# One core, AdaLN + FFN with low-rank experts: the sync engine's loop interleaves row stores with token loads

## What is computed

```python
base   = einsum('btd,od->bto', x, W)                       # conditional layer
logits = einsum('btd,ed->bte', x, Wr) + bias_of_language   # 8 experts, top 2, softmax -> gates
y      = base + 2.0 * einsum('bter,bte,eor->bto', einsum('btd,erd->bter', x, A), gates, B)
z      = einsum('bsi,oi->bso', y, Wf) + b                  # FFN layer
g2     = softmax(einsum('bsi,ei->bse', y, Wrf))            # 4 experts, dense mixture
out    = x + z + einsum('bse,bseo->bso', 2.0 * g2, lora(y))
```

## Time and profile before

| what | value |
|---|---|
| median of 3 runs | 323.39 us (323.33 to 323.43) |
| the profiled execution's own time | 323.47 us |
| its span, first to last instruction | 322.2 us |
| TensorE matmul busy | 318.4 us (99%) |
| VectorE busy | 262.6 us (82%) |
| ScalarE busy | 128.3 us (40%) |
| granted TensorE clock | full in all 40 slices of the span |
| data moved | 27.59 MB, mean 86 GB/s |

### The profile page before, as it was taken

The page is one execution under the profiler, slowest core; times in us unless marked ns, Lnnn a source line. Parts: engine busy times, 40 slices in busy tenths (PEclk is TensorE's granted clock), DMA queues, the critical chain, the costliest instruction groups (busy, mean ns, idle before and its releaser), DMA issues.

```text
span 322.2 us, 5996 instructions
## 1 busy us (share of the span) xinstructions
PE 318.4 (99%) x2246; PEld 312.1 (97%) x2246; DVE 262.6 (82%) x609; ACT 128.3 (40%) x258; POOL 11.3 (3%) x13
## 2 busy tenths in 40 slices
PE   8999999999999999999999999999999999999996
PEld 5999999999999899899999999999999999999996
DVE  4999999798799778988968968878895887888543
ACT  4872846495147236325412503421250350333111
POOL 1001003700000000000000000000000000000000
PEclk9999999999999999999999999999999999999999
DMA  7999000000000312700330150061024006002003
GB/s 273 414 404 287 4 2 0 2 0 2 0 2 0 132 24 46 259 3 0 108 155 1 62 199 0 0 195 65 0 73 187 0 18 241 1 0 110 24 0 130
DMA packets 10705, 27.59 MB, mean 86 GB/s; under 512 B 3167, under 2 KB 4703, under 8 KB 10689
## 3 DMA queue, kind: packets, MB, share of 16 engines
q1 hardware_dynamic: 10256, 26.83, 23.5%
q10 hardware_dynamic: 432, 0.53, 0.5%
HBM read 18.97 MB, written 8.39 MB: 85 GB/s over the span
## 4 chain that ended last, share of the span: by engine, by line
PE 97%; DMA 1%; DVE 0%; ACT 0%; SPq 0%; issue 0%
PE sums L1310 97%; DMA in<-part 1%; PE sums L1559 0%; DVE rows L1069 0%; DVE a_low L800 0%; ACT a_high L549 0%; SPq L444 0%
## 5 line engine op out<-in xcount | busy, mean ns | idle before, releaser
L1310 PE MATMUL sums<-b_high,a_high 128*128 128x256 f32 (+1 forms) x224 | 45.7, 288 | 0.4 <-DVE a_low L800 0.4
L1310 PE MATMUL sums<-b_low,a_high 128*128 128x256 f32 (+1 forms) x224 | 45.3, 285 | 0.0
L1310 PE MATMUL sums<-b_high,a_low 128*128 128x256 f32 (+1 forms) x224 | 45.2, 285 | 0.0
L1310 PEld LDWEIGHTS sums<-b_high,a_high 128*128 128x128 f32 x224 | 34.9, 190 | 1.1 <-DVE a_low L800 0.6
L1310 PEld LDWEIGHTS sums<-b_high,a_low 128*128 128x128 f32 x224 | 34.8, 189 | 0.0
L1310 PEld LDWEIGHTS sums<-b_low,a_high 128*128 128x128 f32 x224 | 34.8, 189 | 0.0
L1310 PE MATMUL sums<-t_high,s_high 128*128 128x354 f32 x96 | 31.3, 326 | 0.0
L1310 PE MATMUL sums<-t_low,s_high 128*128 128x354 f32 x96 | 31.1, 324 | 0.0
L1310 PE MATMUL sums<-t_high,s_low 128*128 128x354 f32 x96 | 31.1, 324 | 0.0
L1069 DVE TENSOR_TENSOR rows<-sums,rows 128x354 f32<-128x354 f32 x48 | 24.4, 522 | 4.1 <-PE sums L1310 3.5
L1310 PE MATMUL sums<-ct_low,st_high 128*128 128x244 f32 (+1 forms) x80 | 25.6, 320 | 0.0
(11 more groups left out here) (151 smaller groups left out, 846.1 us busy)
## 6 DMA issues: line engine op xcount, KB each, us to landing
stage<-tokens SPq DMA_DIRECT2D x14, 512.0 KB, 4.1
out<-rows SPq DMA_DIRECT2D x14, 512.0 KB, 5.0
in<-part SPq DMA_DIRECT2D x7, 585.0 KB, 8.3
in<-part SPq DMA_DIRECT2D x4, 777.0 KB, 14.6
in<-part SPq DMA_DIRECT2D x4, 265.0 KB, 17.1
rows<-tokens SPq DMA_DIRECT2D x2, 512.0 KB, 14.3
out<-rows SPq DMA_DIRECT2D x3, 192.0 KB, 2.3
c_plain<-gate_proj SPq DMA_DIRECT2D x1, 544.0 KB, 19.1
```

Of the source, the lines that this page charges most:

```text
L1310: return nc.tensor.matmul(out_, lhs, rhs, start=start, stop=stop, skip_group_check=True)
```

## The change

SyncE's loop body and the two stores behind the loop are put in another order. Of `load_pair` a `load_tile` is split off, of `store` the two halves become `store_even` and `store_odd`. The loop then issues: load of the even tile, store of the odd tile, load of the odd tile, store of the even tile. Behind the loop pair 6 is stored odd tile first. `store_odd` repeats the wait for `tails_out`, so there is one wait more for each pair. No other engine's program is changed, nor is any transfer's size.

```diff
+            def load_tile(j, odd):
+
+                sp.wait_ge(x_split[odd], j)
+                sp.dma_start(stage[:, odd, :], tokens[2 * j + odd]).then_inc(x_here[odd], 16)
+
             def load_pair(j):
-
                 sp.wait_ge(s_made, 4 * j)
                 for odd in range(2):
-                    sp.wait_ge(x_split[odd], j)
-                    sp.dma_start(stage[:, odd, :], tokens[2 * j + odd]).then_inc(x_here[odd], 16)
-
-            def store(j):
+                    load_tile(j, odd)
+
+            def store_even(j):
                 sp.wait_ge(tails_out, j + 1)
                 sp.wait_ge(a_out, j + 1)
                 sp.wait_ge(c_out, j + 1)
                 sp.dma_start(out[bass.ds(2 * j * P, P), :], rows[:, 0, :]).then_inc(stored[0], 16)
+
+            def store_odd(j):
+                sp.wait_ge(tails_out, j + 1)
                 sp.wait_ge(b_out, j + 1)
                 sp.wait_ge(d_out, j + 1)
                 sp.dma_start(out[bass.ds((2 * j + 1) * P, P), :], rows[:, 1, :]).then_inc(stored[1], 16)
...
             with sp.Fori(0, PAIRS - 2) as j:
-                load_pair(j + 2)
-                store(j)
-            store(PAIRS - 2)
+
+                behind = j + 2
+                sp.wait_ge(s_made, 4 * behind)
+                load_tile(behind, 0)
+                store_odd(j)
+                load_tile(behind, 1)
+                store_even(j)
+            store_odd(PAIRS - 2)
+            store_even(PAIRS - 2)
             store_last(PAIRS - 1)
```

## The result

The median went from 323.29 us to 324.87 us (6 executions each), a ratio of 1.0048 (95% interval 1.0037 to 1.0059). The executions of the changed kernel lie between 324.07 and 325.28 us, those of before between 322.99 and 323.43 us. That is no sign of more scatter in the changed kernel: in the second comparison they lie between 324.03 and 324.84 us (7 executions), those of before between 322.89 and 324.13 us (31). The forecast of 323.05 us (range to 324.0) was wrong, and the rival on the other side, (b), has the place and the sign of what came.

What follows compares the result with a forecast made beforehand. TensorE was taken as the bound, waiting on the odd load's landing. At 4.2 us of landing most of the 0.49 us of stall goes, -0.35 us from 323.47: 323.1 us, or 323.05 on the median's footing; range 322.8 to 324.0.

Steps and rivals of the forecast that it cites:

- (b): Odd load, through S1 to narrow product 3: store in front delays landing by d, costing 5d; 324.9 us at 0.3; chance 0.15.
- What bounds the kernel: TensorE's matmuls, 97.3% of the chain; TensorE hangs on the odd load's landing through VectorE's S1 and narrow sum, without slack.
- The 0.49 us of stall: Ahead of narrow product 3, TensorE's stalls in pairs 3, 5 and 6: 0.17 + 0.15 + 0.17 us.
- The cap on the gain: At narrow product 3, an earlier landing can win at most 0.49 us; a later one costs about 5d, uncapped.
- Step 1: SyncE's queue: odd store issued at about 184.3 instead of 187.29, 3 us earlier, landing at about 187.0 to 187.8.
- Steps 2, 3 and 5: SyncE's odd load issue no later; even load still 4 us ahead if 0.5 us later; stores behind the loop: cost nothing.
- Step 4: Odd load's landing, with one store gone from behind and perhaps a rest in front: 4.2 us instead of 4.4.
- The sign of being wrong: Odd load landing at 4.6 us or more, so that the gaps of five pairs grow together, and the time with them.
- Rival (a): Odd load's landing stays at 4.3 to 4.4 us, front store costing what the back one gave; 323.3 to 323.5 us; chance 0.21.
- The rule of the Trainium skill: Odd load in its ring: strictly, stores behind can't slow it and those in front must; 0 to +1.5 us.

Runs made afterwards that it cites:

- the second comparison: The unchanged changed kernel run once more against the kernel before: median 324.29 us, ratio 1.0030 (1.0019 to 1.0041).
- sum_first_new: Changed kernel, but VectorE makes the narrow sum that narrow product 3 waits for ahead of S1; against the kernel before: 323.36 us, ratio 1.0003.
- before_again: The kernel before, unchanged, run once more for a second trace: 323.49 us, ratio 0.9998.
- no_stores: Old order, both stores of a pair in the loop cut to 16 of 128 rows; against the kernel before: ratio 0.9997.
- new_from_2: SyncE's iterations 0 and 1 peeled off in the old order, new order from iteration 2 on; against the kernel before: 324.10 us, ratio 1.0017.
- only_front: New order, only the even store cut to 16 rows, full odd store in front of the odd load; against the kernel before: ratio 1.0001.
- even_waits_new: Changed order, loop written out, even store waiting for the odd load to land; against the kernel before: 323.28 us, ratio 0.9996.
- stores_wait_old: Old order, loop written out, both stores waiting for the odd load to land; against the kernel before: 323.42 us, ratio 0.9996.
- only_behind: Old order, only the odd store cut to 16 rows, full even store behind the odd load; against the kernel before: ratio 1.0005.

## Why the prediction was wrong, point by point

**What bounds the kernel** held. TensorE hung on the odd load through S1 and the narrow sum, with no slack beyond a landing of 4.2 us; sum_first_new shows that no other path matters by more than 0.12%. The 0.49 us of stall was one execution's: before_again has none. The cap on the gain held as well: no kernel with faster landings, no_stores included, came out more than 0.04% below before.

**Step 1** held: the odd store goes out 1.80 us after the even load (predicted 184.3 - 182.52 = 1.78) and lands after 3.2 us.

**Steps 2, 3 and 5** held. The odd load is issued 3.46 us after the even one in iteration 2, as before (the 185.98 of the working reads 185.97 in the view). The even load lands at 3.5 us there, and nothing waits for `stored`.

**Step 4 is the one that failed**, in "with the even store 0.7 us behind instead of 1.7 I take 4.2 us". Two things were wrong in it. First, it counted on a gain from the store that leaves the load's back. The first store behind costs 0.5 us, the second next to nothing, so there was nothing to win there; in return, the store in front adds 0.2 us where the even store still follows. The load lands at 4.4 to 4.6 us in place of 4.2, and since there is no slack, four pairs stall by up to 0.4 us each. new_from_2, with the new order in these pairs alone, lost 0.55 us. Why the two stores together cost more than the one behind alone stays open. Second, it worked out one iteration, the steady one, and gave the result to all five. In iteration 1 the odd store is 1.06 us ahead, not 1.7, as the order of VectorE's program in pair 1 would have told, and there it costs the load 0.8 to 1.1 us by itself. The 4.8 us of the earlier trace rows, which I noted as scatter, was the landing of the even load of that very iteration, with its late sixteenth. The odd load landed at 5.4 us and TensorE stalled for 0.94 us; what share the instruction packet has in that is not shown.

**Rival (b)** was right in place and sign and wrong in shape. It priced one delay d for five equal pairs. What came was up to 0.4 us of stall in four of them and anything from 0 to 1.2 us in the fifth. The sign of being wrong that the prediction named, a landing of 4.6 us or more, was set too high: almost all landings of pairs 3 to 6 stayed below it, and TensorE stalled all the same. The chance of 0.15 for (b) was too low for a case where the rows themselves showed zero slack and a capped gain.

**Rival (a)**, at 323.3 to 323.5 us, rested on the 4.1 us of the earlier trace rows, and its doubt about that row was the better reading.

**The rule of the Trainium skill.** In "DMA: Bandwidth & Descriptors", section "Queues, rings and completion order", the Trainium skill says that the descriptors of a ring are taken in order. It doesn't say that what stands behind can't slow what stands in front; that was the strict reading of the prediction. The runs contradict that half of it, since a store issued 0.7 us behind costs the load 0.5 us. The other half, that what stands in front must delay, holds where the store lands 2.4 us or more after the load's issue (iterations 0 and 1), and not where it lands 1.5 us after it: only_front has no delay in pairs 3 to 6. The range of 0 to +1.5 us that the prediction gave to that rule did hold the result, for other reasons than the order alone.

## What to carry to other kernels

When a change can win only what a stall costs now but can lose without limit on the same path, an even guess at the disputed duration is a forecast of a loss. Work out a moved transfer's distance to its neighbours for each iteration that has an order of its own, the first ones above all, and take an outlier in a row of landings for a fact about that iteration until it is shown to be scatter. To make a kernel safe against such shifts, take the work that the bounding engine waits for out from behind a wait for a load, or hold stores back until the load has landed: both made the order of this change harmless (1.0003 and 0.9996), though neither was faster than before by more than the noise. Check the stall that you hope to win in a second trace: one execution of before had 0.49 us of it, another none.

## What the runs showed of the hardware that I had not expected

- In pairs 3 to 6 a 512 KB load lands 3.5 us after issue if nothing follows it (even_waits_new, stores_wait_old), and 4.15 us if a 512 KB store is issued 0.7 us behind it on the same queue (only_behind). A later transfer slows an earlier one.
- One read of instructions took 0.9 to 1.7 us of one DMA engine near 157 us, and the even tile load beside it landed in 4.2 to 5.5 us in fifteen of sixteen traces instead of 3.4; that the one causes the other is argued, not shown. In before the load's last packet of 4 bytes came 1.3 us behind its fifteen others.
- TensorE's stalls of 0.14 to 0.21 us ahead of narrow product 3 appear in no list of waits, and longer ones only as "issue"; the starts of the weight loads show them.
- Written out, SyncE's loop issues the odd load 0.02 us after the split that it waits for, as a loop 0.17 us after it.
